# Attention over 2048 rows with a routed feed-forward: where a tile's ranks and the first tile's low parts stand in VectorE's order

## The chip, the core and the metric
One core of one Trainium2 chip runs the whole kernel. The metric is the device time of one execution in microseconds (us). TensorE multiplies matrices, VectorE (DVE) and ScalarE (ACT) work on elements, GpSimd (POOL) does small operations and issues indirect DMAs, SyncE (SP) issues most DMAs. Each runs its own instructions in order and waits on semaphores.

## The reference, cut to what matters
```python
# 2048 rows of 512; E = 8 experts, each row goes to K = 2
x = x + gnn(layernorm(x), adj)     # attention, below
x = x + ffn(layernorm(x))          # shared network + two routed experts
def gnn(s, adj):
    q, k, v = s @ W_q.T + b_q, s @ W_k.T + b_k, s @ W_v.T + b_v
    z = q @ k.T / sqrt(512) * adj
    z = where(z == 0, -10000, z)
    return relu(softmax(z, axis=1) @ v)
def ffn(X):
    w = softmax(X @ Wr); topk_w, topk_idx = top_k(w, 2); topk_w = softmax(topk_w)
    return shared(X) + sum over the two experts of topk_w * expert(X)
```

## The kernel before, in words
The attention is done for 16 tiles of 128 rows. Its products are split: each operand has a high part (`_h`, a rounded copy made by ScalarE) and a low part (`_l`, the rest, made by VectorE), and three matmuls stand for one (`PASSES`). Step i is `attention_step(j, b)` with i = 2j + b. Each engine has a function of that name, and the order in which these functions issue their work is written out by hand; the steps 2 to 13 run in a loop over j, the others are written out.

In step i TensorE computes the scores of tile i + 1 in four chunks of 512 columns (`scores`), then, in even steps with b = 0, the queries of the next two tiles, and then the weighted values of tile i in four groups (`attend`, which wait for `pT_l`). Between the chunks of the scores it does small things for tiles i - 1 in the router: after chunk 0 `count_picks(i - 1)`, after chunk 1 `turn_normalised(i)` (L861, waits for `x2row`), after chunk 2 `route_logits(i)` (L867, waits for `x2T`). Here "tile i" of the router is the tile whose attention was finished in step i - 1.

VectorE's step starts with `output` and `residual` (the row that attention leaves, its variance `var_e`), `take_counts`, and `row_normalised`, which needs `rstd` from GpSimd. Then for tile i + 1, whose scores stand in PSUM: `mask` (multiplies a chunk by the adjacency, L1586), `fill_zeros` (puts -10000 where it is zero and keeps the maximum, L1594 and L1598), and among them `low(i, 0)` and `low(i, 1)` (the low parts of tile i's transposed probabilities, L1450, which wait for ScalarE's `high`). After the fourth chunk come `row_max` (L1604), `logits`, `ranks(i - 1)` (L1696 to L1701), the queries' scaling, `turn_squares(i + 1)` (the 32x32 transposes of the probabilities, L1612, after ScalarE's exponentials), and the router's `picks` and `pick_weights`.

The transposed probabilities make a round trip: SyncE writes `turned` to HBM and reads it back with its blocks moved (`move`), and loads the next adjacency between. ScalarE's step is `high(i, 0)` (waits for the round trip), `keep_turned` (writes `x2T`), `high(i, 1)`, and the exponentials of tile i + 1 after its row maximum.

`ranks` gives each row its place in its two experts' regions. GpSimd's `scatter` waits for it (semaphore `routing`), casts the places (L675) and issues four indirect DMAs (L683, L685), which send the normalised row and its weight to the regions. GpSimd's order in the loop is:
```python
power_of_row(2 * j + 1, 0)
scatter(2 * j, 1)
power_of_row(2 * j + 2, 1)
scatter(2 * j + 1, 0)
```
and `power_of_row(n)` waits until the scatter of tile n - 2 has landed (semaphore `sent`) before it computes `rstd` (L650). In step 0 there is no router work (`prev` is false); `counted`, which governs `ranks` and `take_counts`, is true from step 2 on. The last step is written out by itself.

Of the kernel before, what the change touches and what calls it, by code (L numbers as in the profile page):

```python
# [18 lines left out]
def gnn_moe(nc, x, adj, w_q, b_q, w_k, b_k, w_v, b_v, w_r, wg_s, wu_s, wd_s, wg, wu, wd, out):  # L19
# [46 lines left out]
    with ExitStack() as ctx:  # L66
# [198 lines left out]
        def sem(name):  # L265
            if name not in sems:
                sems[name] = ctx.enter_context(nc.semaphore(name))
            return sems[name]

        def wait(eng, name, value):  # L270

            if isinstance(value, int) and value <= 0:
                return
            eng.wait_ge(sem(name), value)

        def wait_apart(eng, name, value):


            wait(eng, name, value)
            if not isinstance(value, int):  # L280
                eng.sem_inc(sem(f"waits_{eng.engine.name}"), 1)
# [8 lines left out]
        def moved_half(h):  # L290
            return turned[:, h, :, :].rearrange("p i (k q) -> p k i q", q=Q)


        def half(x_, h):
            return x_[:, HALF * h:HALF * h + HALF, :].rearrange("p k (i q) -> p k i q", q=Q)
# [15 lines left out]
        def queries_follow(j, b):  # L311

            return b == 0 and (not isinstance(j, int) or j + 1 < NT // 2)
# [1134 lines left out]
        def _(dve):  # L1448
            def minus(o, a, b):
                return dve.tensor_tensor(o, a, b.bitcast(F32), ALU.subtract)  # L1450
# [129 lines left out]
            def mask(i, b, n):  # L1580

                dve.wait_ge(sem("scores"), 4 * i + n + 1)
                if n % 2 == 0:
                    wait(dve, f"adj_in{n // 2}", 16 * (i + 1))
                part = sc[:, n * 512:(n + 1) * 512]
                dve.scalar_tensor_tensor(out=part, in0=bank[n][:], scalar=s_q[:, bass.ds(i, 1)], in1=part, op0=ALU.add, op1=ALU.mult  # L1586
                                         ).then_inc(sem("scored"), 1)

            def fill_zeros(i, b, n):

                part = sc[:, n * 512:(n + 1) * 512]
                dve.wait_ge(sem("scored"), 4 * i + n + 1)
                wait(dve, "filled", 4 * i + n)
                dve.tensor_scalar(fill[:], part, 0.0, MASKED, ALU.is_equal, ALU.mult).then_inc(sem("zeros"), 1)  # L1594
                if n == 0:
                    wait(dve, "nmx_done", i)
                wait_apart(dve, "zeros", 4 * i + n + 1)
                dve.tensor_tensor_reduce(out=part, in0=part, in1=fill[:], scale=1.0, scalar=-3.0e38, op0=ALU.add,  # L1598
                                         op1=ALU.max, accum_out=mx4[:, n:n + 1]).then_inc(sem("filled"), 1)
# [16 lines left out]
            def low(i, h):  # L1616
                dve.wait_ge(sem("pT_h"), 2 * i + h + 1)
                minus(half(pT["l"], h), moved_half(h), half(pT["h"], h)).then_inc(sem("pT_l"), 1)

            def last_group(g):  # L1620
                dve.wait_ge(sem("pT_h"), TURNED + g + 1)
                part = slice(4 * g, 4 * g + 4)
                minus(pT["l"][:, part, :].rearrange("p k q -> p (k q)"), bank[4 + g % 2][:],
                      pT["h"][:, part, :].rearrange("p k q -> p (k q)")).then_inc(sem("pT_l"), 1)


            def output(i, b, o=bank[6]):

                wait(dve, "exp_done", i)
                wait(dve, "o_done", i - 1)  # L1630
                dve.reciprocal(rden[:], den[:, 1 - b:2 - b]).then_inc(sem("rden_done"), 1)
                wait(dve, "attended", 4 * i)
                wait(dve, "x1_out", 16 * (i - 1))
                wait(dve, "x2_done", i - 1)
                wait(dve, "rden_done", i)
                dve.scalar_tensor_tensor(out=x1[:], in0=o[:], scalar=rden[:, 0:1], in1=bv_row[:], op0=ALU.mult,
                                         op1=ALU.add).then_inc(sem("o_done"), 1)

            def residual(i, b, n):

                dve.wait_ge(sem(f"xr_in{1 - b}"), n * 16)
                wait(dve, "o_done", i)
                dve.scalar_tensor_tensor(out=x1[:], in0=x1[:], scalar=0.0, in1=x_t[:, 1 - b, :], op0=ALU.max,
                                         op1=ALU.add).then_inc(sem("x1_done"), 1)
                wait(dve, "x1_done", i)
                statistics(x1[:], NT + i, 1 - b)

            def row_normalised(i, b):

                wait(dve, "x2_turned", i - 2)  # L1650
                normalise(x2row[1 - b][:], x1[:], NT + i, 1 - b).then_inc(sem("x2_done"), 1)
# [9 lines left out]
            def then_route(i, ins):  # L1661
                steps[0] += 1
                ins.then_inc(sem("routing"), 1)
                wait_apart(dve, "routing", (i - 1) * ROUTER + steps[0])
# [23 lines left out]
            def take_counts(i):  # L1688
                wait(dve, "counted", i)
                dve.tensor_copy(counts[:], bank[7][:, 0:2 * E]).then_inc(sem("counts_read"), 1)  # L1690

            def ranks(i):

                steps[0] = ROUTER - 4
                wait(dve, "counts_read", i)
                then_route(i, dve.tensor_tensor(rank[:], counts[:, 0:E], base[:], ALU.add))  # L1696
                for k in range(2):
                    then_route(i, dve.tensor_tensor_reduce(out=rsel[:], in0=route[:, k * E:(k + 1) * E], in1=rank[:], scale=1.0,
                                                           scalar=0.0, op0=ALU.mult, op1=ALU.add,
                                                           accum_out=route[:, 2 * E + k:2 * E + k + 1]))  # L1700
                then_route(i, dve.tensor_tensor(base[:], base[:], counts[:, E:2 * E], ALU.add))  # L1701
                assert steps[0] == ROUTER and RANKED == ROUTER - 1

            def attention_step(j, b, last=False, prev=True, split=False):
                i = 2 * j + b
                if last:
                    last_group(0)
                    last_group(1)
                    output(i, b)
                    take_counts(i - 1)  # L1710
                    ranks(i - 1)
                    residual(i, b, j + b)
                    last_group(2)
                    row_normalised(i, b)
                    last_group(3)
                    first_pieces(2, 3)
                    first_pieces(3, 4)
                    logits(i)
                    picks(i)
                    pick_weights(i)  # L1720
                    return
                counted = prev and not (isinstance(i, int) and i == 1)
                ahead = queries_follow(j, b)
                if prev:
                    output(i, b)
                    residual(i, b, j + b)
                    if counted:
                        take_counts(i - 1)
                    row_normalised(i, b)
                mask(i + 1, 1 - b, 0)  # L1730
                mask(i + 1, 1 - b, 1)
                fill_zeros(i + 1, 1 - b, 0)
                if prev:
                    low(i, 0)
                fill_zeros(i + 1, 1 - b, 1)
                mask(i + 1, 1 - b, 2)
                if prev:
                    low(i, 1)
                fill_zeros(i + 1, 1 - b, 2)
                mask(i + 1, 1 - b, 3)  # L1740
                fill_zeros(i + 1, 1 - b, 3)
                row_max(i + 1, 1 - b)
                if prev:
                    logits(i)
                else:

                    low(i, 0)
                    low(i, 1)
                if counted:
                    ranks(i - 1)  # L1750
                if ahead:
                    scaled_queries(2 * j + 2, 0)
                if split:
                    first_pieces(0, 2)
                else:
                    turn_squares(i + 1)
                if ahead:
                    queries_low(2 * j + 2, 0)
                    scaled_queries(2 * j + 3, 1)
                if prev:  # L1760
                    picks(i)
                if ahead:
                    queries_low(2 * j + 3, 1)
                if prev:
                    pick_weights(i)
# [352 lines left out]
```

## Time and profile before
| | |
|---|---|
| time, median of 3 runs | 1401.52 us (1401.38 to 1402.24) |
| profiled execution, its own time | 1403.48 us |
| its span | 1401.8 us |
| TensorE busy (matmuls) | 1372.9 us, 98% |
| VectorE busy | 908.3 us, 65% |
| ScalarE busy | 453.4 us, 32% |
| GpSimd busy | 191.0 us, 14% |
| mean granted TensorE clock | 0.994 of full speed |

The span goes from the first to the last instruction; the time has what lies around it too. The attention's steps lie between about 90 and 530 us. A busy share is a mean over stages with different limits.

### The profile page before, as it was taken

What the parts mean: (1) busy time and instruction counts of PE and PEld (TensorE: products, weight loads), DVE (VectorE), ACT (ScalarE), POOL (GpSimd) and SP (SyncE); (2) the same over time, 40 slices, a digit from 0 to 9 for tenths busy, and PEclk for the clock granted to TensorE, in tenths of its full rate; (3) what the DMA queues carried; (4) which work ended last, traced back from release to release, by engine and by line L of the source; (5) the groups of instructions that cost most, each with busy time, mean ns of one, the idle gap of its engine ahead of it and who ended that gap; (6) DMA issues with size and microseconds to landing.
All of it is one profiled execution on the core that took longest, in us unless ns stands there. A gap on an engine that the chain in (4) does not pass through costs nothing.

```text
span 1401.8 us, 19781 instructions
## 1 busy us (share of the span) xinstructions
PE 1372.9 (98%) x6720; PEld 1181.9 (84%) x6720; DVE 908.3 (65%) x1957; ACT 453.4 (32%) x702; POOL 191.0 (14%) x234
## 2 busy tenths in 40 slices
PE   9998999999999999999999999999999999999998
PEld 7887887787787878898898989898898989888887
DVE  7956766766676666646575747657375745367874
ACT  4522212121122134434242514324242424243331
POOL 3500011112111223021102010100101020200000
PEclk9999999999999999999999999999999999999999
DMA  5806467546644587164435225261354444453101
GB/s 183 251 26 185 126 176 182 139 127 188 177 145 127 164 248 255 62 161 136 120 110 158 83 46 203 39 200 33 65 175 87 147 110 139 126 167 105 46 16 60
DMA packets 114420, 185.47 MB, mean 132 GB/s; under 512 B 13776, under 2 KB 47568, under 8 KB 114336
## 3 DMA queue, kind: packets, MB, share of 16 engines
q1 hardware_dynamic: 98064, 153.43, 35.4%
q0 software_dynamic: 9760, 18.93, 7.2%
q10 hardware_dynamic: 6528, 12.22, 3.1%
q8 instruction: 41, 0.67, 0.2%
q14 instruction: 27, 0.22, 0.0%
HBM read 129.82 MB, written 55.77 MB: 132 GB/s over the span
## 4 chain that ended last, share of the span: by engine, by line
PE 64%; DVE 1%; DMA 1%; issue 1%; POOL 0%; ACT 0%; DVEq 0%; POOLq 0%
PE bank L305 58%; PE bank L1035 5%; PE bank L1026 1%; DMA owners<-owner,idx 1%; DVE z L1898 0%; PE bank L987 0%; PE bank L867 0%; POOL slots L683 0%; PE bank L845 0%; PE bank L861 0%; DVE pT_l L1450 0%; DVE fill L1594 0%; POOL owners L685 0%; DVE sc L1586 0%; DVE hT_l L1450 0%
## 5 line engine op out<-in xcount | busy, mean ns | idle before, releaser
L1823 DVE TENSOR_TENSOR hid<-bank,hid 128x384 f32<-128x384 f32 (+1 forms) x80 | 46.8, 585 | 176.0 <-PE bank L305 175.8
L305 PE MATMUL bank<-dn_h,hT_h 128*128 128x512 f32 x320 | 125.7, 393 | 0.2 <-DVE hT_l L1450 0.2
L305 PE MATMUL bank<-dn_h,hT_l 128*128 128x512 f32 x320 | 125.8, 393 | 0.0
L305 PE MATMUL bank<-dn_l,hT_h 128*128 128x512 f32 x320 | 125.5, 392 | 0.0
L305 PE MATMUL bank<-xq_h,gate_h 128*128 128x384 f32 (+1 forms) x320 | 111.3, 348 | 0.1
L305 PE MATMUL bank<-xq_h,gate_l 128*128 128x384 f32 (+1 forms) x320 | 111.2, 347 | 0.0
L305 PE MATMUL bank<-xq_l,gate_h 128*128 128x384 f32 (+1 forms) x320 | 110.8, 346 | 0.0
L305 PE MATMUL bank<-xq_h,up_h 128*128 128x384 f32 (+1 forms) x320 | 110.7, 346 | 0.0
L305 PE MATMUL bank<-xq_h,up_l 128*128 128x384 f32 (+1 forms) x320 | 110.4, 345 | 0.0
L305 PE MATMUL bank<-xq_l,up_h 128*128 128x384 f32 (+1 forms) x320 | 110.4, 345 | 0.0
L1121 ACT ACTIVATE hT_h<-hid 128x384 fp32r<-128x384 f32 (+1 forms) x96 | 53.8, 561 | 164.2 <-DVE hid L1823 124.7
L305 PE MATMUL bank<-xnT_h,yT_h 128*128 128x512 f32 x256 | 105.8, 413 | 0.0
L305 PE MATMUL bank<-v_h,pT_h 128*128 128x512 f32 x256 | 101.5, 397 | 3.7 <-DVE pT_l L1450 3.7
L305 PE MATMUL bank<-xnT_l,yT_h 128*128 128x512 f32 x256 | 101.7, 397 | 0.0
L305 PE MATMUL bank<-xnT_h,yT_l 128*128 128x512 f32 x256 | 101.5, 396 | 0.0
L305 PE MATMUL bank<-v_l,pT_h 128*128 128x512 f32 x256 | 100.9, 394 | 0.0
L305 PE MATMUL bank<-v_h,pT_l 128*128 128x512 f32 x256 | 100.7, 393 | 0.0
L711 POOL DMA_INDIRECT acc<-y,q_owner x24 | 40.9, 1704 | 356.1 <-ACT y L1121 295.5
L1299 ACT ACTIVATE hid<-bank 128x384 f32<-128x384 f32 (+1 forms) x80 | 41.1, 513 | 144.0 <-PE bank L305 144.0
L1121 ACT ACTIVATE pT_h<-turned 128x1024 fp32r<-128x1024 f32 x30 | 31.7, 1058 | 153.8 <-DMA turned<-p_moved 153.8
L1450 DVE TENSOR_TENSOR hT_l<-hid,hT_h 128x384 fp32r<-128x384 f32 (+1 forms) x96 | 57.6, 600 | 33.9 <-ACT hT_h L1121 33.6
L1850 DVE STREAM_TRANSPOSE xq_raw<-e_x 32x256 f32<-32x256 f32 (+1 forms) x192 | 70.8, 369 | 2.9
(277 smaller groups left out, 3294.3 us busy)
## 6 DMA issues: line engine op xcount, KB each, us to landing
sc<-in_adj_dram SPq DMA_DIRECT2D x32, 512.0 KB, 7.1
gate_raw<-in_L_ffn_Wg_dram SPq DMA_DIRECT2D x16, 1024.0 KB, 5.5
up_raw<-in_L_ffn_Wu_dram SPq DMA_DIRECT2D x16, 1024.0 KB, 10.1
dn_raw<-in_L_ffn_Wd_dram SPq DMA_DIRECT2D x16, 1024.0 KB, 12.6
p_moved<-turned SPq DMA_DIRECT2D x30, 512.0 KB, 7.5
turned<-p_moved SPq DMA_DIRECT2D x120, 128.0 KB, 4.7
x_t<-in_x_dram SPq DMA_DIRECT2D x24, 256.0 KB, 5.0
slots<-x2row ACTq DMA_DIRECT2D x12, 512.0 KB, 4.4
```

Source lines behind the costliest of these rows:

```text
L305: mm = pe.matmul(o, lhs(a, c), rhs(b, c), start=first and n == 1, stop=last and n == 3 * len(chunks))
L711: pool.indirect_dma_start(acc, bass.IndirectOffsetOnAxis(ap=at_, axis=0), y[b % 2][:, k, :], None, compute_op=ALU.add).then_inc(sem("added ...
L1026: mm = pe.transpose(bank[5 + f][:, c * P:(c + 1) * P], hid[:, f, c * P:(c + 1) * P], ident[:])
L1035: mm = pe.matmul(bank[4][:], hT[a][:, f, c * P:(c + 1) * P], dn[(a0, a1)[f] % 3][b_][:, c, :], start=f == 0 and n == 0, stop=f == 1 and n ...
L1121: return act.activation(o, i, ACT.Copy) if scale is None else act.activation(o, i, ACT.Copy, scale=scale)
L1299: act.activation(hid[:, c % 2, 0:w], bank[c % 2][:, 0:w], ACT.Silu).then_inc(sem("silu"), 1)
L1450: return dve.tensor_tensor(o, a, b.bitcast(F32), ALU.subtract)
L1823: dve.tensor_tensor(hid[:, c % 2, 0:w], bank[2 + c % 2][:, 0:w], hid[:, c % 2, 0:w], ALU.mult).then_inc(sem("hid"), 1)
L1850: return dve.transpose(o[32 * a:32 * a + 32, :, :].rearrange("p c (k q) -> p k c q", k=n)[:, :, :, 32 * i:32 * i + 32], rows_[32 * i:32 * ...
```

## The change
In VectorE's `attention_step`, `ranks(i - 1)` moves from behind the row maximum and the logits of the step to directly behind the second of the four masks. In step 0, `low(0, 0)` and `low(0, 1)` move from behind the row maximum of tile 1 to the places that they have in all other steps, behind the first fill and behind the third mask. No operation is added or removed, and the last step is as it was.
```diff
                 mask(i + 1, 1 - b, 0)
                 mask(i + 1, 1 - b, 1)
+                if counted:
+
+                    ranks(i - 1)
                 fill_zeros(i + 1, 1 - b, 0)
-                if prev:
-                    low(i, 0)
+                low(i, 0)
                 fill_zeros(i + 1, 1 - b, 1)
                 mask(i + 1, 1 - b, 2)
-                if prev:
-                    low(i, 1)
+                low(i, 1)
                 fill_zeros(i + 1, 1 - b, 2)
                 mask(i + 1, 1 - b, 3)
                 fill_zeros(i + 1, 1 - b, 3)
                 row_max(i + 1, 1 - b)
                 if prev:
                     logits(i)
-                else:
-
-                    low(i, 0)
-                    low(i, 1)
-                if counted:
-                    ranks(i - 1)
```

## Rows read from the trace of the kernel before
**Rows 1.** The page, busy time of each engine.
```profile
PE 1372.9 (98%) x6720; PEld 1181.9 (84%) x6720; DVE 908.3 (65%) x1957; ACT 453.4 (32%) x702; POOL 191.0 (14%) x234
```
**Rows 2.** Waits of TensorE: in all, times, longest.
```profile
PE bank L861 <- DVE x2row L1462: 16.8, 6, 3.4
```
**Rows 3.** Timeline of TensorE, an even step: start, duration, [idle before <- releaser].
```profile
320.59 0.39 PE L305 MATMUL bank<-xnT_h,yT_h 128*128 128x512 f32 x1
...
328.93 0.66 PE L861 MATMUL bank<-ident,x2row 128*128 128x128 f32 x4 [2.50 <-DVE x2row L1462]
...
332.18 0.95 PE L867 MATMUL bank<-w_r_sb,x2T 128*128 128x8 f32 x8
```
**Rows 4.** Timeline of VectorE, an odd step and the next even one.
```profile
301.10 0.55 DVE L1462 TENSOR_SCALAR x2row<-x,mv,rstd 128x512 f32<-128x512 f32 x1 [0.68 <-POOL rstd L650]
...
303.03 0.75 DVE L1586 SCALAR_TENSOR_TENSOR sc<-bank,s_q,sc 128x512 f32<-128x512 f32 x1 [0.72 <-PE bank L305]
...
312.44 0.16 DVE L1604 TENSOR_REDUCE nmx<-mx 128x1 f32<-128x4 f32 x1
...
314.86 2.37 DVE L1612 STREAM_TRANSPOSE turned<-sc 128x1024 f32<-128x1024 f32 x2 [0.86 <-ACT sc L1203]
...
324.20 0.15 DVE L1458 TENSOR_SCALAR var_e<-mv 128x1 f32<-128x1 f32 x1
...
328.33 0.55 DVE L1462 TENSOR_SCALAR x2row<-x,mv,rstd 128x512 f32<-128x512 f32 x1 [3.90 <-POOL rstd L650]
```
**Rows 5.** Timeline of GpSimd, the same steps.
```profile
313.85 0.20 POOL L675 CAST idx<-route 128x2 int32<-128x2 f32 x1 [12.86 <-DVE route L1698]
...
315.11 1.04 POOL L683 DMA_INDIRECT slots<-x2row,idx  x1 [0.82 <-POOL owner L678]
...
327.66 0.57 POOL L650 TENSOR_TENSOR rstd<-var_e,neg_half 128x1 f32<-128x1 f32 x1 [7.70 <-DMA owners<-owner,idx]
```
**Rows 6.** Windows of three even steps: length, busy by engine, clock, DMA share, GB/s.
```profile
206.89:239.76 32.87, 29.43 (x159) 25.20 (x158) 20.75 (x57) 6.46 (x10) 5.13 (x8) 1.00 0.69 183
263.21:297.13 33.92, 31.00 (x159) 26.41 (x158) 20.92 (x57) 6.45 (x10) 5.13 (x8) 0.95 0.67 180
...
490.46:517.49 27.03, 24.70 (x122) 20.41 (x120) 18.86 (x52) 9.01 (x13) 5.96 (x8) 1.00 1.01 303
```
**Rows 7.** Timeline of VectorE, the ranks of an even step.
```profile
283.16 0.16 DVE L1696 TENSOR_TENSOR rank<-counts,base 128x8 f32<-128x8 f32 x1
...
284.69 0.88 DVE L1554 TENSOR_SCALAR y_f<-bank,c 128x256 f32<-128x256 f32 x2 [0.33 <-DVE base L1701]
```
**Rows 8.** Timeline of ScalarE, high parts that wait for the round trip.
```profile
112.78 1.06 ACT L1121 ACTIVATE pT_h<-turned 128x1024 fp32r<-128x1024 f32 x1 [12.83 <-DMA turned<-p_moved]
...
131.79 1.06 ACT L1121 ACTIVATE pT_h<-turned 128x1024 fp32r<-128x1024 f32 x1 [9.37 <-DMA turned<-p_moved]
...
161.47 1.06 ACT L1121 ACTIVATE pT_h<-turned 128x1024 fp32r<-128x1024 f32 x1 [11.10 <-DMA turned<-p_moved]
...
216.66 1.06 ACT L1121 ACTIVATE pT_h<-turned 128x1024 fp32r<-128x1024 f32 x1 [11.44 <-DMA turned<-p_moved]
...
498.51 1.06 ACT L1121 ACTIVATE pT_h<-turned 128x1024 fp32r<-128x1024 f32 x1 [9.74 <-DMA turned<-p_moved]
```
**Rows 9.** Timeline of TensorE, steps 0 to 2.
```profile
115.98 0.80 PE L305 MATMUL bank<-v_h,pT_h 128*128 128x512 f32 x1 [3.71 <-DVE pT_l L1450]
...
138.56 0.95 PE L867 MATMUL bank<-w_r_sb,x2T 128*128 128x8 f32 x8
...
163.07 1.06 PE L867 MATMUL bank<-w_r_sb,x2T 128*128 128x8 f32 x8 [0.90 <-ACT x2T L1121]
```
**Rows 10.** Timeline of VectorE, steps 0 and 1.
```profile
117.81 2.37 DVE L1612 STREAM_TRANSPOSE turned<-sc 128x1024 f32<-128x1024 f32 x2
...
137.41 1.22 DVE L1450 TENSOR_TENSOR pT_l<-turned,pT_h 128x1024 fp32r<-128x1024 f32 x1
```
**Rows 11.** DMA from 314.86 to 328.66: queue, packets, MB, share of 16 engines.
```profile
q0 software_dynamic: 224, 0.53, 14.1%
```

## The prediction
> **What bounds the kernel now.** I read the page's busy table first: TensorE is busy for 98% of the span [rows 1], so an edit on VectorE can only pay where TensorE waits for it. The wait table then names those places: the largest single item is the transposes of the normalised rows (L861), which stood still 16.8 us in six waits for VectorE's `row_normalised` [rows 2]. The timelines say why. I call a step even when it has b = 0 (it also computes queries) and odd when b = 1, and T the moment at which TensorE starts the scores of an even step; in the step shown T is 320.59 [rows 3]. VectorE has the variance at 324.20, but `x2row` starts only at 328.33 after 3.90 us of idleness behind GpSimd's `rstd` [rows 4]; GpSimd in turn stood behind a DMA, the scatter of the previous tile (`power_of_row` waits for it), until 327.66 [rows 5]. In an odd step the same wait is 0.68 us [rows 4]. The scatter was late because its addresses come from `ranks`, which VectorE makes behind the last mask: GpSimd's cast follows at 313.85 [rows 5].
>
> The loss also has a second half. An even step with 3.4 us of idleness took 32.87 us, of which 29.43 busy; another needed 31.00 busy at a mean granted clock of 0.95 [rows 6]: part of it ran at the lower of the two levels, 1.2 GHz, after the idle time. Three of the six (start 263, 376, 434) show this, 31.00 - 29.43 = 1.57 us each. Loss of the six: 16.8 + 3 x 1.57 = 21.5 us. That is the most this part can give.
>
> **Part 1, `ranks` behind the second mask.** In an odd step the second mask starts at 303.03 [rows 4]; ranks would start about 0.7 us later, and the address is ready a little over 1 us after that, at about 304.9, instead of 313.8 [rows 5]: 9 us earlier. The hold to be removed is 3.2 us (0.68 of the 3.90 is there in any case). So the scatter has landed long before the next `power_of_row`, by 5 us or more, and the six holds go: **-21.5 us**.
>
> What it costs: `ranks` is four small operations, each waited for. From its first to the next operation behind it goes 284.69 - 283.16 = 1.5 us [rows 7]. Behind `logits` this lay beside ScalarE's exponentials: the 128x1024 transposes start 2.42 us after the row maximum in an odd step and waited for ScalarE for 0.86 of it [rows 4]. Behind the second mask there is no such cover in an odd step: from 303.03 to the row maximum at 312.44 VectorE runs masks, fills and low parts without a pause that the timeline attributes to another engine, so the row maximum comes 1.5 us later, and so do the exponentials, the transposes, the round trip over HBM, the picks and the next step's `output`. In an even step VectorE has idle time there (it waits for scores, whose chunks end later), and the 1.5 us are hidden; if not, the low parts still lie some 8 us ahead of the attends, behind 5.7 us of queries.
>
> Two things then reach TensorE late in the next even step.
> First, `x2row`: the variance is ready at T + 3.61, now T + 5.1; `x2row` starts 0.9 after it when nothing holds it (T + 6.0), and TensorE 0.6 after that (328.33 to 328.93 [rows 3, 4]): T + 6.6. TensorE is there at 328.93 - 2.50 - 320.59 = T + 5.8 [rows 3]. A stall of **0.8 us** in place of 2.8 on average.
> Second, `x2T`: TensorE's router product needs ScalarE's copy, which is queued behind `high(i, 0)`, and that waits for the round trip. The six landings lie at T + 9.77 (216.66, the first, T = 206.89) to T + 8.05 (498.51, the last, T = 490.46), mean T + 8.7 [rows 6, 8]. With 1.5 more, T + 10.2. From the start of `high` to the router product goes 163.07 - 161.47 = 1.6 us [rows 8, 9]: T + 11.8. TensorE, unheld, is there at 332.18 - 2.50 - 320.59 = T + 9.1 [rows 3]. So an even step loses 2.7 us in all (the 0.8 is part of it), and the six lose **16.2 us**. The wait moves from the scatter to the round trip; it does not vanish.
>
> What the emptied DMA queue gives back: transposes start at 314.86 = T - 5.7 [rows 4], so the round trip takes 8.7 + 5.7 = 14.4 us with the scatter in it. In step 1, where there was no scatter yet, it took 131.79 - 117.81 = 13.98 us [rows 8, 10]. That says 0.4. The scatter's queue held 14.1% of the engines over a trip of 13.8 us [rows 11], which says at most 1.9. Moved earlier, it falls between 305 and 316 in this trace, where next to no DMA runs. I take 0.5 us for each even step, nearer to the measured trip: **-3.0 us**; ends 0 and -11.
>
> The clock: a stall of 0.90 us left it at its upper level [rows 9], while of two steps with 32.87 - 29.43 = 3.44 and 33.92 - 31.00 = 2.92 us of idleness only the second fell [rows 6]. With 0.8 and 1.4 us apart from each other I expect one fall in six, **+1.6 us**; ends 0 and 4.7.
>
> **Part 2, the first tile's low parts among tile 1's masks.** Now `low(0, 0)` can start when ScalarE's high part ends, 112.78 + 1.06 = 113.84 [rows 8], instead of 114.7, and TensorE starts attending at 115.1 instead of 115.98 [rows 9]: 0.8 us earlier. But VectorE now stands at that wait with three fills and two masks of tile 1 behind it. From 113.87: low 1.15, fill 1.16, mask 0.67, low 1.15, fill 1.16, mask 0.67, fill 1.16 (the spacings in this step), which ends at about 121.0. Row maximum 121.1, transposes 2.4 later at 123.4 instead of 117.81 [rows 10]: 5.6 us late. The queries' low parts end about 5.3 behind the transposes' start, at 128.8; TensorE needs them after its attends, at 129.1, so they are just hidden. The landing moves from 131.79 to 123.4 + 13.98 = 137.4, and the router product of step 1 from 138.56 to 137.4 + 1.6 = 139.0 [rows 8, 9]: the gain of 0.8 has become a loss of 0.4. Next, `low(1, 0)`, at 137.41 [rows 10], has to wait for a high part that ends at 138.45: 1.0 us late, and this runs on through row maximum, transposes and landing of tile 2, whose router product was already waiting (0.90 us [rows 9]). **+1.1 us** in all; if the trip takes a microsecond less, 0; if 15 us, +2.1.
>
> **The sum.** -21.5 + 16.2 - 3.0 + 1.6 + 1.1 = -5.6 us. The profiled execution took 1403.48 us (span 1401.8), 2 us above the median of the runs; the difference is applied to the median: 1401.5 - 5.6 = **1396 us**. All later stages are TensorE's and only start earlier. A difference under 0.2% (2.8 us) can hardly be told from none.
>
> **Rivals.**
> A: *the round trip shrinks by the scatter's full share*, 1.9 us each. Then an even step loses only the 0.8 of `x2row`: -21.5 + 4.9 + 1.1 = -15.5, **1386 us**. For it: the scatter takes part of the queues through much of the trip [rows 11]. Against: the trip without a scatter was only 0.4 shorter.
> B: *the delay eats the gain*. No relief and the clock falls in three of six: -21.5 + 16.2 + 4.7 + 1.1 = +0.5, **1402 us**. For it: landings as they were, and falls in three of six before.
> C, the other side: *the scatter, moved beside VectorE's fills, holds them up*. Before, it ran beside transposes and small operations; now its four issues of some 1.0 us [rows 5] fall between fills and low parts of an odd step, which is the chain just found tight. If three fills each wait for one issue, 3.1 us are added to each odd step and the six even ones lose as much: +19, **1414 us**. It decides from 0.9 us per odd step on (5.6/6). No row has a fill beside a scatter; the transposes beside it kept their length. The Trainium skill speaks for it: its page "SBUF — State Buffer", section "Who interferes with whom", says that VectorE in a two-port mode and GpSimd take a shared port pair for whole instructions, and that the first to issue blocks the other. No trace here shows either outcome.
> D: *the first tile costs more*: a slower trip, plus a clock fall at step 1's new stall. +3 to +4 us there, sum near -3, **1399 us**.
>
> **How the numbers follow.** Forecast (-3 to -9 us) 0.45; A and what lies between 0.17; B 0.21; C 0.11; D 0.06. Faster: forecast, A and a little of D, 0.63; within 0.2%: most of B, the rest of D, 0.20; slower: C and B's upper part, 0.17. The range 1388 to 1403 leaves out A's far end and C.
>
> **What would show it.** In the trace after: GpSimd's `rstd` waits for VectorE's variance only, with no DMA wait; the cast in odd steps some 8 us after the step's start in place of 16.7; row maximum in odd steps 1.5 us later relative to the second mask. In even steps TensorE waits 0.8 us before L861 and 1 to 2.5 us before L867 for ScalarE's `x2T`. In the first tile the wait for `pT_l` is 2.9 in place of 3.7 us, and step 1 has a new wait at L867. I am wrong if L867 never waits (A), if fills last longer than 0.42 us or start late beside GpSimd (C), or if VectorE hides `ranks` in odd steps after all, which would give 9 us more.

## The result and the profile after

| | before | after |
|---|---|---|
| median, us | 1401.88 (4 runs, 1401.38 to 1408.26) | 1384.51 (4 runs, 1383.97 to 1386.81) |
| span of the profiled execution, us | 1401.8 | 1382.3 |
| TensorE busy, us | 1372.9 | 1367.2 |
| mean granted TensorE clock | 0.994 | 0.999 |

The ratio is 0.9869, 95% interval 0.9838 to 0.9899: 17.4 us faster. The forecast had 5.6 us, and its range ended at 1388. The sign was right; the size was a third of what came.

The page's busy row of the kernel after, to be read beside [rows 1]:
```profile
PE 1367.2 (99%) x6720; PEld 1177.1 (85%) x6720; DVE 909.4 (66%) x1957; ACT 452.6 (33%) x702; POOL 197.1 (14%) x234
```
TensorE has the same 6720 matmuls but is busy 5.7 us less. As the work did not change, the difference is one of clock. The rest of the 19.5 us by which the span fell is time in which it stood still. Its waits (us in all, times, longest):
```profile
PE bank L861 <- DVE x2row L1462: 3.9, 6, 0.8
PE bank L305 <- DVE pT_l L1450: 2.5, 2, 2.1
...
PE bank L867 <- ACT x2T L1121: 0.7, 1, 0.7
PE bank L305 <- DVE yT_l L1450: 0.7, 1, 0.7
```
The six holds at L861 fell from 16.8 us [rows 2] to 3.9. The wait that the forecast put in their place, at L867 for ScalarE's `x2T`, occurs once, in step 2, where the kernel before had it too (0.90 us [rows 9]). None of the six even steps that had been held has it.

The windows of three even steps and of the last step, each from the start of its scores (columns as in [rows 6]):
```profile
204.97:235.16 30.19, 29.42 (x159) 25.21 (x158) 21.71 (x62) 6.34 (x10) 5.54 (x8) 1.00 0.68 199
258.59:288.73 30.14, 29.43 (x159) 25.20 (x158) 21.73 (x62) 6.34 (x10) 5.54 (x8) 1.00 0.68 201
312.19:342.51 30.32, 29.60 (x160) 25.13 (x158) 21.73 (x62) 6.34 (x10) 5.55 (x8) 1.00 0.69 200
473.08:499.00 25.92, 25.30 (x123) 20.91 (x122) 19.98 (x58) 9.00 (x13) 6.27 (x8) 1.00 1.00 308
```
An even step now takes 30.1 to 30.3 us, of which 29.4 to 29.6 are busy at full clock, where it took 32.87 and 33.92 [rows 6]. Idleness of 0.7 us in place of 3.44 and 2.92 leaves the clock at its upper level, 2.4 GHz.

VectorE's timeline, the odd step before T = 312.19 and the next even one (start, duration, [idle before <- releaser]), beside [rows 4, 7]:
```profile
294.62 0.75 DVE L1586 SCALAR_TENSOR_TENSOR sc<-bank,s_q,sc 128x512 f32<-128x512 f32 x1 [0.71 <-PE bank L305]
295.29 0.16 DVE L1696 TENSOR_TENSOR rank<-counts,base 128x8 f32<-128x8 f32 x1
...
296.73 0.43 DVE L1594 TENSOR_SCALAR fill<-sc 128x512 f32<-128x512 f32 x1 [0.22 <-DVE base L1701]
...
305.47 0.16 DVE L1604 TENSOR_REDUCE nmx<-mx 128x1 f32<-128x4 f32 x1
...
317.24 0.15 DVE L1458 TENSOR_SCALAR var_e<-mv 128x1 f32<-128x1 f32 x1
...
318.15 0.55 DVE L1462 TENSOR_SCALAR x2row<-x,mv,rstd 128x512 f32<-128x512 f32 x1 [0.68 <-POOL rstd L650]
```
The ranks cost 296.73 - 295.29 = 1.44 us. From the second mask to the row maximum it is 305.47 - 294.62 = 10.85 us, where it was 312.44 - 303.03 = 9.41 [rows 4]: the same 1.44, not hidden. `x2row` waits for `rstd` 0.68 us and no longer 3.90.

In an even step the ranks are not hidden there either. The masks and the row maximum of the even step before the change, and then after it, with the start of the odd step ahead of it:
```profile
328.79 1.40 DVE L1586 SCALAR_TENSOR_TENSOR sc<-bank,s_q,sc 128x512 f32<-128x512 f32 x2
...
338.86 0.16 DVE L1604 TENSOR_REDUCE nmx<-mx 128x1 f32<-128x4 f32 x1
```
```profile
289.13 0.75 DVE L1636 SCALAR_TENSOR_TENSOR x<-bank,rden,bv_row 128x512 f32<-128x512 f32 x1 [1.91 <-PE bank L305]
...
318.62 1.41 DVE L1586 SCALAR_TENSOR_TENSOR sc<-bank,s_q,sc 128x512 f32<-128x512 f32 x2
...
330.17 0.16 DVE L1604 TENSOR_REDUCE nmx<-mx 128x1 f32<-128x4 f32 x1
```
From the masks to the row maximum it is 330.17 - 318.62 = 11.55 us, where it was 338.86 - 328.79 = 10.07, and VectorE does not wait for a chunk of the scores in between. TensorE is not held by this, since VectorE has time to spare later: it still waits 1.91 us for TensorE at the start of the odd step (289.13), and all six waits at L861 are in even steps.

GpSimd's timeline of the same steps, beside [rows 5]:
```profile
296.36 0.20 POOL L675 CAST idx<-route 128x2 int32<-128x2 f32 x1 [3.76 <-DVE route L1698]
...
297.62 1.31 POOL L683 DMA_INDIRECT slots<-x2row,idx  x1 [0.82 <-POOL owner L678]
...
317.48 0.57 POOL L650 TENSOR_TENSOR rstd<-var_e,neg_half 128x1 f32<-128x1 f32 x1 [14.47 <-DVE var_e L1458]
```
The cast starts 296.36 - 288.73 = 7.6 us into the odd step, and `rstd` waits only for the variance. Then TensorE, beside [rows 3], and ScalarE, beside [rows 8], in the even step:
```profile
318.76 0.66 PE L861 MATMUL bank<-ident,x2row 128*128 128x128 f32 x4 [0.72 <-DVE x2row L1462]
...
322.10 1.06 PE L867 MATMUL bank<-w_r_sb,x2T 128*128 128x8 f32 x8
```
```profile
320.50 1.06 ACT L1121 ACTIVATE pT_h<-turned 128x1024 fp32r<-128x1024 f32 x1 [8.57 <-DMA turned<-p_moved]
321.47 0.58 ACT L1121 ACTIVATE x2T<-bank 128x512 f32<-128x512 f32 x1
```
Here the data of the round trip arrives at 320.50 = T + 8.3 although its row maximum came 1.44 us later; at T = 204.97 it arrives at T + 7.7. Before, it was T + 8.7 on average. `x2T` ends at 322.05, and TensorE takes it at 322.10 without a wait. So the trip itself has become shorter. I measure it from the start of VectorE's transposes to ScalarE's first `pT_h`: in this step it is 320.50 - 307.88 = 12.62 us. The mean of the six trips that begin in odd steps is 12.08, and was 14.42 in the trace before, 2.3 us more.

### The profile page after: what moved, and what is told of

It reads as the page before. It is cut to its first block, busy times and chain, and to the rows that moved or that the text cites. A ratio compares the mean times of both kernels' runs of the same rounds, so it can differ in the third digit from the quotient of the medians.

```text
span 1382.3 us, 19780 instructions
## 1 busy us (share of the span) xinstructions
PE 1367.2 (99%) x6720; PEld 1177.1 (85%) x6720; DVE 909.4 (66%) x1957; ACT 452.6 (33%) x702; POOL 197.1 (14%) x234
## 4 chain that ended last, share of the span: by engine, by line
PE 82%; issue 8%; DVE 4%; DMA 3%; POOL 2%; ACT 1%; SPq 1%; POOLq 0%; DVEq 0%; ACTq 0%
PE bank L305 74%; PE bank L1035 5%; DMA owners<-owner,idx 2%; DMA turned<-p_moved 1%; POOL slots L683 1%; PE bank L1026 1%; DMA p_moved<-turned 1%; ACT sc L1203 1%; SPq L452 1%; PE bank L867 0%; POOL owners L685 0%; PE bank L791 0%; PE bank L745 0%; DVE fill L1594 0%; DVE pT_l L1450 0%
## 6 DMA issues: line engine op xcount, KB each, us to landing
dn_raw<-in_L_ffn_Wd_dram SPq DMA_DIRECT2D x16, 1024.0 KB, 12.5
```

## The experiments

Two theories were left. S: the scatter, when it falls into the round trip, is what makes the trip long, and the change took it out of there. V: trips vary by themselves from one execution to the next, and the forecast's step was right on average. Kernels that ran together share the runs of the kernel before: 1402.61 us (17 runs) for the first four, 1402.03 (23) for the next four, 1403.25 (9) for the last three. In all of them "trip" is the mean of the six that begin in odd steps.

| kernel | median, us (runs) | ratio, 95% interval | trip, us | L861 wait, us | L867 wait, us |
|---|---|---|---|---|---|
| before_again | 1403.11 (1) | | 14.29 | 16.9 | 0.6 |
| after_again | 1384.62 (1) | | 12.06 | 3.8 | 1.2 |
| ranks_only | 1384.46 (4) | 0.986, 0.9844 to 0.9876 | 11.84 | 3.8 | 0.8 |
| lows_only | 1403.35 (12) | 1.0005, 0.9992 to 1.0019 | 14.53 | 17.5 | 0.7 |
| copy_in_trip | 1399.60 (8) | 0.9977, 0.9963 to 0.9990 | 14.12 | 3.9 | 10.4 |
| copy_rows | 1383.84 (2) | 0.9866, 0.9846 to 0.9885 | 12.16 | 3.9 | 0.8 |
| copy_weights | 1402.96 (8) | 1.0001, 0.9983 to 1.0019 | 14.73 | 3.9 | 13.1 |
| late_send | 1400.97 (10) | 0.9987, 0.9974 to 1.0001 | 13.72 | 14.1 | 1.2 |
| before_no_weights | 1379.18 (5) | 0.9832, 0.9806 to 0.9858 | 12.93 | none | 0.4 |
| ranks_first | 1380.56 (5) | 0.9842, 0.9816 to 0.9868 | 11.96 | none | 0.6 |
| ranks_first_lows | 1379.96 (5) | 0.9836, 0.9810 to 0.9862 | 12.06 | none | 0.8 |

### The two kernels once more, and each part alone

`before_again` and `after_again` are the two kernels with no edit.

> The kernel before once more, on the chip of the three runs beside it. Theory S (the round trip over HBM got shorter because the scatter left it): the trips of the even steps last 13.8 to 15.5 us from VectorE's transposes to ScalarE's high part, as in the first profile, and the trips of tiles 0 and 1, which have no scatter in either kernel, last the same as in the changed kernel on this chip. Theory V (trips differ from one execution or chip to another, and the change has nothing to do with it): trips of tiles 0 and 1 differ from those of the changed kernel by as much as the later ones, some 1 to 2 us.

> The changed kernel once more, beside the kernel before on one chip. Theory S: trips that end in an even step 11.5 to 12.6 us, those of tiles 0 and 1 as long as in the kernel before; no wait for x2T in even steps; about 1384 us. Theory V: all trips shift together against the first profile, and the difference between tile 0's trip and the later ones is the same in both kernels.

The trips repeat within 0.13 us of the first profiles (14.42 and 14.29, 12.08 and 12.06), so V falls. The wait at L867 in step 1 that the forecast had for part 2 is in this second profile of the kernel after, not in the first, where the same line starts unheld at 136.73:
```profile
137.62 1.06 PE L867 MATMUL bank<-w_r_sb,x2T 128*128 128x8 f32 x8 [0.70 <-ACT x2T L1121]
```

`ranks_only` puts step 0's low parts back; `lows_only` puts the ranks back.
```diff
# ranks_only, against after
-                low(i, 0)
+                if prev:
+                    low(i, 0)
...
-                low(i, 1)
+                if prev:
+                    low(i, 1)
...
                     logits(i)
+                else:
+                    low(i, 0)
+                    low(i, 1)
# lows_only, against after
                 mask(i + 1, 1 - b, 1)
-                if counted:
-                    ranks(i - 1)
...
                     logits(i)
+                if counted:
+                    ranks(i - 1)
```


> Only the ranks moved; tile 0's low parts stay behind tile 1's row maximum. If the gain is the six holds (21.5 us less 0.7 us for each of six even steps, 3.9 in all): 17 to 18 us faster than before, about 1384. My prediction's 1.1 us for the low parts would make this 1 us faster than the whole change; if instead the low parts are what gained the 1.9 us that the changed kernel is ahead at the start of step 4, this is 2 us slower than the whole change, about 1386.5.

> Only tile 0's low parts moved; ranks stay behind the logits. By my prediction +1.1 us; by the first profile after, -1.9 us; in both cases the six holds stay, so within 3 us of the kernel before. If the low parts carried the gain, it would be 17 us faster.

The ranks are the whole gain, and the low parts make no difference that can be told: the interval of `lows_only` goes from 1.1 us faster to 2.7 us slower.

### The scatter put back into the trip, without its waits

GpSimd scatters a second time into spare tensors, right after the row maximum of each step, while the kernel's own scatter stays where the change put it. `rstd` does not wait for this copy, so that the holds at L861 stay away and only the effect on the trip is seen. `copy_in_trip` copies both kinds, `copy_rows` the rows of 2 KB alone, `copy_weights` the weights alone (8 bytes for each row). The loop's first and last pair are written out; the copies run for the scatters of tiles 2 to 13.
```diff
+            def copy_scatter(n, b):
+                wait_apart(pool, "nmx_done", n + 3)
+                for k in range(2):
+                    place = idx[:, 2 * b + k:2 * b + k + 1]
+                    # in copy_in_trip and copy_rows:
+                    pool.indirect_dma_start(slots_2, bass.IndirectOffsetOnAxis(ap=place, axis=0),
+                                            bv_row[:], None).then_inc(sem("tail_added"), 16)
+                    # in copy_in_trip and copy_weights:
+                    pool.indirect_dma_start(owners_2, bass.IndirectOffsetOnAxis(ap=place, axis=0),
+                                            owner[:, b, k, :], None).then_inc(sem("tail_added"), 16)
...
                 power_of_row(2 * j + 1, 0)
+                wait_apart(pool, "tail_added", 64 * (2 * j - 2))
                 scatter(2 * j, 1)
+                copy_scatter(2 * j, 1)
```


> The changed kernel with its early scatter, and in steps 3 to 13 a second scatter of the same size (two of 256 KB rows, two of 1 KB weights, the rows taken from the bias row) into two tensors that nothing reads, issued when the next tile's row maximum is there: where the scatter stood before the change, but nothing waits for it in time. Theory S (the scatter in the trip is what made the trip long): trips that end in an even step go back from 12.1 to 14.3 us; then my arithmetic of the x2T path applies, 14.3 - 5.7 + 1.5 + 1.6 = T + 11.7 against T + 9.1, so TensorE waits 1.5 to 2 us for x2T behind a wait of 0.7 for x2row, a loss of 2.6 us in each of five or six even steps instead of 0.7: 10 to 12 us slower than the changed kernel, 1394 to 1397. Rival W (the trip got shorter for another reason, such as ranks no longer standing between row maximum and transposes): trips stay at 12, and the time within 2 us of the changed kernel.

With both kinds the trip is back at 14.12 us and `x2T` is late (the waits of TensorE):
```profile
PE bank L892 <- ACT x2T L1146: 10.4, 8, 3.2
PE bank L886 <- DVE x2row L1487: 3.9, 6, 0.8
```
That is the picture of the forecast, with its wait of 0.8 and a later one for `x2T`, and S holds. The time, 1399.6, is 15 us above the kernel after, more than the 10 to 12 expected: the waits had been counted, and the lower clock not. TensorE is busy for 1373.7 us here, 6.5 more than in the kernel after. That 1399.6 lies near the first forecast of 1396 says little, since this kernel has no holds and a second scatter. Which half of the scatter does it was the next question.

> As the run with the second scatter, but its two DMAs of rows only, without the two of weights. If the bytes in the queues are the cause (0.52 MB), trips of 14.0 to 14.3 us and nearly the same time as with all four. If it is the number of DMAs and their completions, half of the lengthening.

> As the run with the second scatter, but its two DMAs of weights only (2 x 128 pieces of 8 bytes). If bytes are the cause, trips stay at 12.1 us and the time is that of the changed kernel. If small writes or completions hold the queues, trips of 13 us or more.

The rows cost nothing: 1383.84 us and a trip of 12.16, as with no copy at all. The weights cost everything: a trip of 14.73 and 1402.96, all that the change had gained. SyncE's timeline of one trip shows where. First `copy_rows`: the write of the first half (`p_moved<-turned`) and the first read back (`turned<-p_moved`), which waits for the write to be complete.
```profile
309.55 0.33 SPq L448 DMA_DIRECT2D p_moved<-turned  x1
...
312.59 5.56 SPq L454 DMA_DIRECT2D turned<-p_moved  x8
```
Then `copy_weights`:
```profile
316.44 0.33 SPq L448 DMA_DIRECT2D p_moved<-turned  x1
...
322.26 4.42 SPq L454 DMA_DIRECT2D turned<-p_moved  x8
```
From write to read it is 3.0 us in the first and 5.8 in the second. SyncE's waits from 180 to 500 us give the sum, `copy_rows` first:
```profile
SPq L454 <- DMA p_moved<-turned: 22.5, 22, 1.6
```
```profile
SPq L454 <- DMA p_moved<-turned: 52.1, 22, 5.2
```
The queue share would have told the opposite. These are GpSimd's queue in the trip of `copy_rows` from 308.27 to 320.90 and in that of `copy_weights` from 315.17 to 329.40 (packets, MB, share of 16 engines):
```profile
q0 software_dynamic: 160, 0.52, 10.9%
```
```profile
q0 software_dynamic: 64, 0.00, 0.4%
```
So 2 x 128 writes of 8 bytes, with next to no share in the queues, hold up the completion of SyncE's writes, and the reads behind them. The Trainium skill, "DMA: Bandwidth & Descriptors", section "Queues, rings and completion order", says that a semaphore's increment is a strongly ordered write, which lands only after every earlier write of that DMA engine, across its queues. By that rule an increment of SyncE's write stands behind the small writes in GpSimd's queue; the trace agrees, with 5.8 us in place of 3.0. That this ordering is the mechanism is argued from it, not shown. Rows and weights have the same number of pieces, 2 x 128. They differ in the size of a piece and in how close together the pieces land, and no run here tells these two apart.

The copies do not stand quite where the scatter stood. `copy_weights` issues its first one 2.7 us ahead of SyncE's first write (316.44), and in the kernel before the first weights went out 0.3 us behind it:
```profile
313.71 0.96 POOL L694 DMA_INDIRECT owners<-owner,idx  x1 [3.41 <-DVE nmx L1627]
```
```profile
316.13 0.33 SPq L446 DMA_DIRECT2D p_moved<-turned  x1
...
316.46 0.96 POOL L685 DMA_INDIRECT owners<-owner,idx  x1 [0.30 <-issue]
```
So the copies show what such writes can do, and what they did in the kernel before has to be read from a kernel with the scatter in its old place. That is `before_no_weights`, below.

### The holds put back, and the weights left out

`late_send` holds the scatter itself until the row maximum (without the hold for the last three tiles).
```diff
-            def scatter(n, b):
+            def scatter(n, b, held=True):
+                if held:
+                    wait(pool, "nmx_done", n + 3)
```


> The changed kernel, but GpSimd starts each scatter only when the next tile's row maximum is there: VectorE's order as changed, the scatter as late as before, and 1.4 us later still. The holds come back: TensorE waits 3 to 5 us for x2row in each even step, more than before the change by the 1.4 us of the ranks, and the clock falls in three or more: 1407 to 1413, slower than before. If the holds stayed away, the gain would come from VectorE's order and not from the scatter's time.

The holds came back, but smaller, and without the forecast's full price. TensorE's waits:
```profile
PE bank L865 <- DVE x2row L1466: 14.1, 6, 2.9
...
PE bank L871 <- ACT x2T L1125: 1.2, 2, 0.7
```
GpSimd's timeline says why the expected time was missed:
```profile
312.49 0.18 POOL L675 CAST idx<-route 128x2 int32<-128x2 f32 x1 [13.29 <-DVE nmx L1608]
...
313.74 1.04 POOL L683 DMA_INDIRECT slots<-x2row,idx  x1 [0.82 <-POOL owner L678]
...
325.77 0.57 POOL L650 TENSOR_TENSOR rstd<-var_e,neg_half 128x1 f32<-128x1 f32 x1 [7.20 <-DMA owners<-owner,idx]
```
The row maximum was at 312.08, and the first send 1.66 us behind it, where it was 315.11 - 312.44 = 2.67 us in the kernel before [rows 4, 5], which also had to make the ranks in between. The scatter starts a microsecond earlier within the trip, and its end, which `rstd` waits for, comes earlier: `rstd` starts 11.3 us after the transposes (314.50), where it was 327.66 - 314.86 = 12.8 us. I had put it where the kernel before has it. The two waits, at L861's place and at L867's, also do not add: TensorE, once held for `x2row`, comes later to `x2T`.

`before_no_weights` is the kernel before, without the two DMAs that send a tile's weights (L685). This leaves out a part of the computation: the weights in the regions keep their first value, and the experts' rows are added with a weight of 0.
```diff
-                    pool.indirect_dma_start(owners, bass.IndirectOffsetOnAxis(ap=place, axis=0),
-                                            owner[:, b, k, :], None).then_inc(sem("sent"), 16)
...
-                wait_apart(pool, "sent", 64 * (n - 2))
+                wait_apart(pool, "sent", 32 * (n - 2))
```


> The kernel before, without the scatter's two DMAs of weights (256 pieces of 8 bytes for a tile); the rows are still sent, and as late as before. The regions' weights keep their first value, so all experts' results are added with weight 0 to the spare rows. If these small writes are what holds the DMA engines (the run with only weights in the trip says so, the run with only rows says that rows are harmless): trips that end in an even step 12.1 us, the rows land before the next variance is ready, the holds at x2row go or shrink under 1 us, and with the 1.4 us of ranks not in VectorE's chain the kernel takes 1378 to 1383 us. If the rows' own landing is the hold, as my prediction had it, the holds stay at 2 us or more and the time is above 1392.

It takes 1379.18 us with the ranks still in their old place. All waits at L861 are gone, and GpSimd's `rstd` waits for the variance, with the rows sent as late as ever:
```profile
304.69 1.04 POOL L683 DMA_INDIRECT slots<-x2row,idx  x1 [0.82 <-POOL owner L678]
306.04 0.96 POOL L683 DMA_INDIRECT slots<-x2row,idx  x1 [0.30 <-issue]
314.02 0.57 POOL L650 TENSOR_TENSOR rstd<-var_e,neg_half 128x1 f32<-128x1 f32 x1 [7.03 <-DVE var_e L1456]
```
So both losses of the kernel before, the holds and much of the long trip, go with these writes. For the holds, `before_again` shows how late the scatter's DMAs land (median us from issue to landing, 180 to 500 us):
```profile
slots<-x2row,idx POOLq DMA_INDIRECT x22, 5.0
owners<-owner,idx POOLq DMA_INDIRECT x22, 8.2
```
Without the weights the last row DMA is also issued 2.5 us sooner after the first than the last weights were.

For the trip, the landing of SyncE's two writes, first in `before_again` (issued at 316.15 and 317.27) and then in `before_no_weights` (305.72 and 306.84):
```profile
p_moved<-turned SPq DMA_DIRECT2D x1, 512.0 KB, 3.5
p_moved<-turned SPq DMA_DIRECT2D x1, 512.0 KB, 7.3
```
```profile
p_moved<-turned SPq DMA_DIRECT2D x1, 512.0 KB, 3.5
p_moved<-turned SPq DMA_DIRECT2D x1, 512.0 KB, 6.5
```
In the six trips the first write lands at 3.5 to 3.6 us in both kernels, and the second at 7.3 to 8.4 with the weights and 6.4 to 6.5 without. In the kernel before it is thus the second write whose landing comes later with these weights, and with the second row DMA, which goes out 1.3 us later behind them. The copy in `copy_weights`, issued earlier, also holds up the first. The trip, 12.93 us, is 1.5 us shorter than in the kernel before and still 0.9 above that of the kernel after, where the first write lands at 3.0. What makes up this rest, the late rows or their issues, was not told apart. That rows cost nothing is shown only for the place of `copy_rows`, issued ahead of SyncE's first write.

### A better place for the ranks

In the kernel after VectorE stands still for 0.71 us before the second mask (294.62 above), waiting for a chunk of the scores. Ranks made in front of that mask use this time.
```diff
                 mask(i + 1, 1 - b, 0)
-                mask(i + 1, 1 - b, 1)
                 if counted:
                     ranks(i - 1)
+                mask(i + 1, 1 - b, 1)
```
`ranks_first_lows` does the same, with step 0's low parts in their old place as in `ranks_only`.

> The changed kernel with ranks one place earlier, between the first and the second mask. There VectorE waits 0.71 us for the second chunk of scores in an odd step, so half of the 1.44 us of ranks is covered; TensorE's wait for x2row in the even steps (0.7 us in five, 0.2 in one) goes to 0.0 to 0.1: 3 to 4 us faster than the changed kernel, 1380 to 1381.5. If the wait comes from something else, no change.

> As the run with ranks between the masks, and tile 0's low parts back behind tile 1's row maximum. The two runs before differed by nothing that can be measured in this part, so the same again: within 2 us of the kernel with ranks between the masks.

The timeline of VectorE in `ranks_first`, in an odd step:
```profile
292.38 0.16 DVE L1696 TENSOR_TENSOR rank<-counts,base 128x8 f32<-128x8 f32 x1
...
293.81 0.75 DVE L1586 SCALAR_TENSOR_TENSOR sc<-bank,s_q,sc 128x512 f32<-128x512 f32 x1 [0.22 <-DVE base L1701]
```
The mask no longer waits for TensorE. The ranks should delay the row maximum by about 1.44 - 0.71 = 0.7 us and no more; from the first mask to the row maximum it is 11.49 us here, 12.31 in the kernel after and 10.88 in the kernel before. About that much TensorE had been waiting at L861, and all six waits are gone. The median is 1380.56 us, beside 1384.51 of the kernel after (other chip runs, each by its ratio to the kernel before: 0.9842 and 0.9869, with intervals that overlap). The six waits of 3.9 us are the expected difference. The medians differ by as much, but with these intervals the time alone does not show it; the waits do. The low parts again make none: with them TensorE's wait for `pT_l` is 1.8 us in `ranks_first` and 3.4 in `ranks_first_lows`, but the first has a wait of 2.3 for `yT_l`, which the second has not.

## Why the prediction was wrong in size, step by step

**The loss of the six holds, -21.5 us: right.** 16.8 us of waiting went to 3.9, and the 5.7 us of busy time show the low clock gone (the forecast had 3 x 1.57 = 4.7).

**Ranks, 1.5 us in each odd step, not hidden there: right. Hidden in the even ones: wrong reason, right outcome.** They take 1.44 us in an odd step. In an even step VectorE was to have idle time between the second mask and the row maximum; it has none, and the row maximum comes 1.48 us later there too. It costs nothing because VectorE waits for TensorE at the start of the next odd step. `x2row`'s stall of 0.8: right, 0.72 in the step shown. The order of the cast, 8 us into the step: 7.6.

**`What the emptied DMA queue gives back`, -3.0 us: this step failed.** It took 0.5 us off the trip for each even step, and the trips shrank by 14.42 - 12.08 = 2.3, more than its own upper end of 1.9. With 2.3 the data land at T + 8.7 + 1.44 - 2.3 = T + 7.8, where T + 7.7 and T + 8.3 were read, and the router product can start 1.6 us later, at T + 9.9 at the latest. TensorE comes there at T + 9.1 + 0.7 = T + 9.8. So the second part of the forecast delay, 2.7 - 0.8 = 1.9 us in each of six steps, does not occur, and neither does the clock fall that hung on it. For the delay, the relief and the clock together the forecast charged 16.2 - 3.0 + 1.6 = 14.8 us; the runs show 6 x 0.65 = 3.9. The sum is then -21.5 + 3.9 = -17.6 us; measured, -17.4. That the two agree so closely is partly luck: the spans of the two profiles differ by 19.5 us, since the clock gave back 5.7 in place of 4.7 and the other waits of TensorE shrank by 0.7; the profiled run of the kernel before was 1.6 us above its median.

Two readings had led to 0.5. The first was one trip without a scatter, that of tile 1 with 13.98 us, the longest of its kind: in the profiles of this study the same trip took from 12.5 to 13.98, and in `before_again`, the same kernel, 12.54. The mean of six was set beside a single trip in a stage of its own. The second was the scatter's share of the queues, 14.1% [rows 11], as the upper end. The share says how long the engines move a queue's bytes; `copy_weights` has 0.4% and lengthens the trip by 2.6 us, `copy_rows` has 10.9% and leaves it as it is.

**The clock, +1.6 us: went with the stall.** The four windows shown above have a clock of 1.00, and the mean over the span is 0.999.

**Part 2, +1.1 us: too small to be told from 0.** TensorE's wait for `pT_l` went from 3.71 [rows 9] to 2.08, somewhat better than the forecast 2.9. Step 1's new wait at L867 is in one profile of two, 0.70 us, and the queries' low parts, "just hidden" in the forecast, were late by as much (`yT_l`, 0.7 us). `lows_only` at 1.0005 is 0.7 us slower, with an interval from -1.1 to +2.7 us, which holds both 0 and the forecast.

**Rivals.** A came out in place and nearly in size (1386 us), but not by its reason, the queue's share. B needed the delay, which did not occur. C fell: the scatter does run beside VectorE's fills now, and they take 0.42 us as before (0.43 at 296.73). It is GpSimd's issues that last longer, with 1.31 us for the first in place of 1.04 [rows 5], and nothing waits for them; that VectorE's work beside them is the cause is argued from the coincidence. The page "SBUF — State Buffer" of the Trainium skill, section "Who interferes with whom", has the two block one another; of that the trace agrees with the one direction at most. D did not occur: step 1's stall is 0.70 us at most, and the clock from 130 to 170 us is 1.00.

## What to carry to other kernels

Price a DMA that moves to another place by how small its pieces are and by whose completion falls beside them, not by its bytes or its queue's share; then look at the transfers that ran beside it as well as at those who wait for it. To say what such a transfer costs another, copy it into spare memory at the place in question, one kind at a time, with nobody waiting for the copy. Put the copy at the same distance from its neighbours, or check it by taking the original out: here a copy issued 3 us earlier held up the first write, which the original did not. When small chained operations are moved, put them where the engine has an idle time in front of a wait: 0.7 us of cover were one line away.

## What the runs showed of the hardware that was not expected

256 indirect writes of 8 bytes, 2 KB in all, lengthened a trip of 12.1 us over HBM and back to 14.7, while 256 rows of 2 KB, 0.52 MB, sent at the same place by the same queue left it at 12.2. One completion of another queue's 512 KB write came at 5.8 us with the small writes beside it, and at 3.0 with the large ones. In the kernel before, where the small writes were issued just behind that write, it came at 3.5 us with them or without, and the next write's completion moved instead, from 6.5 us to 7.3 and more.
